# Three buffers instead of two for the stacked queries of a cross-attention stage

## The reference

```
x = layernorm(x + self_part(x))      # causal exp(q k^T) row sums, then a 1 -> 16 -> 512 MLP
x = layernorm(x + cross(x))          # 16 heads of 32, 154 keys per sequence
x = layernorm(x + ffn(x))            # int16-like activations, int8-like weights, 512 -> 2048 -> 512

cross: q, k, v = heads(x), heads(ctx), heads(ctx)
       weights = softmax((q k^T + bias) / sqrt(32)); out = (weights v) @ w_out
```

## Time and profile before

| | |
|---|---|
| median of 3 runs | 2299.92 us (2289.78 to 2301.79) |
| profiled execution | 2294.64 us |
| its span, first to last instruction | 2292.8 us |
| busy PE / DVE / ACT / POOL | 2126.1 / 1737.9 / 1086.0 / 827.0 us |
| share of the chain that ended last: PE / DVE / DMA / ACT | 82% / 6% / 4% / 2% |
| of it the DMA `qs<-stack` | 3% |
| mean granted TensorE clock | 0.947 |

### The profile page before, as it was taken

How to read it: one execution, slowest core, us unless ns; L and a number is a source line. 1 busy time by engine, 2 the same in 40 slices (tenths; PEclk the granted TensorE clock), 3 DMA queues, 4 the chain that set the end, 5 groups by cost and what they waited for, 6 DMA issues and landing times.

```text
span 2292.8 us, 32921 instructions
## 1 busy us (share of the span) xinstructions
PE 2126.1 (93%) x11880; PEld 1185.0 (52%) x11904; DVE 1737.9 (76%) x3296; ACT 1086.0 (47%) x1522; POOL 827.0 (36%) x802
## 2 busy tenths in 40 slices
PE   7999999984998999999999859999999699999997
PEld 3444444431776777777777624444444344444443
DVE  6768686865677897898898665777666488888885
ACT  1444444442454555555555324444444465555551
POOL 2122221222134555455555342222222134444442
PEclk9999999996588999999999779999999899999999
DMA  6344343457769979989995437888888656667662
GB/s 232 107 132 148 99 145 107 115 137 187 172 147 181 269 165 201 265 182 180 262 193 141 155 84 255 287 283 288 271 268 273 244 200 232 225 227 235 227 224 79
DMA packets 386626, 448.46 MB, mean 196 GB/s; under 512 B 279270, under 2 KB 279430, under 8 KB 368032
## 3 DMA queue, kind: packets, MB, share of 16 engines
q1 hardware_dynamic: 322448, 286.07, 46.4%
q0 software_dynamic: 64016, 160.28, 22.6%
HBM read 258.93 MB, written 138.73 MB: 173 GB/s over the span
## 4 chain that ended last, share of the span: by engine, by line
PE 82%; DVE 6%; issue 5%; DMA 4%; ACT 2%; POOL 1%; SPq 0%; DVEq 0%; POOLq 0%; ACTq 0%
PE ps_h L1704 19%; PE ps L1947 19%; PE ps_proj L600 10%; PE ps_o L1272 8%; PE ps_w L1301 6%; PE ps_s L620 5%; PE ps_o L1268 3%; DMA qs<-stack 3%; PE ps_m L1224 3%; PE ps_m L1226 3%; PE ps_l L1250 3%; DVE rope_t L428 1%; PE ps_t L1286 1%; PE ps_l L1247 1%; DVE x_hi L411 1%
## 5 line engine op out<-in xcount | busy, mean ns | idle before, releaser
L1704 PE MATMUL ps_h<-xT,b_rows 128*128 128x512 f16 x2048 | 444.5, 380 | 12.7 <-DMA xT<-x_lo 12.7
L1947 PE MATMUL ps<-w,g_hi 128*128 128x512 f16 x1024 | 389.1, 380 | 21.7 <-DVE g_lo L1883 21.7
L1947 PE MATMUL ps<-w,g_lo 128*128 128x512 f16 x1024 | 389.0, 380 | 0.0
L1704 PEld LDWEIGHTS ps_h<-xT,b_rows 128*128 128x128 f16 x2048 | 200.8, 98 | 256.1 <-issue 16.0
L1272 PEld LDWEIGHTS ps_o<-vm,pT 128*128 128x128 f32 x2048 | 308.9, 208 | 14.7
L1545 ACT ACTIVATE h<-ps_h,b_in_sb,col_scale 128x512 f32<-128x512 f32 x256 | 199.5, 779 | 240.8 <-PE ps_h L1704 240.6
L1096 DVE TENSOR_REDUCE stack<-ps_m 128x2 f16<-128x308 f32 x512 | 244.1, 478 | 78.1 <-PE ps_m L1226 75.9
L1272 PE MATMUL ps_o<-vm,pT 128*128 128x33 f32 x2048 | 292.4, 269 | 0.0
L1047 ACT ACTIVATE pT<-logit 128x512 f32<-128x512 f32 x320 | 199.2, 624 | 131.0 <-DVE logit L1114 130.0
L1618 DVE TENSOR_REDUCE amax_t<-h 128x1 f32<-128x2048 f32 x64 | 146.2, 2284 | 118.3 <-ACT h L1545 118.1
L1796 POOL TENSOR_TENSOR rstd<-vare,minus_half 128x1 f32<-128x1 f32 x64 | 154.3, 2411 | 208.4 <-DVE vare L1901 208.4
(11 more groups left out here) (179 smaller groups left out, 3935.5 us busy)
## 6 DMA issues: line engine op xcount, KB each, us to landing
hidden<-h POOLq DMA_DIRECT2D x64, 1024.0 KB, 6.8
hT<-hidden SPq DMA_DIRECT2D x64, 1024.0 KB, 6.1
xc<-x_cols SPq DMA_DIRECT2D x16, 1024.0 KB, 5.1
xr<-x_rows SPq DMA_DIRECT2D x16, 1024.0 KB, 5.5
x_rows<-x POOLq DMA_DIRECT2D x16, 1024.0 KB, 4.8
x1t<-x_rows SPq DMA_DIRECT2D x64, 256.0 KB, 3.8
bt_main<-bias_main SPq DMA_DIRECT2D x16, 1024.0 KB, 6.9
xres<-x_rows SPq DMA_DIRECT2D x64, 256.0 KB, 3.8
```

What stands on the lines that cost most here:

```text
L1704: mm = pe.matmul(ps_h[f % 4][:], w1[:, c, f * P:(f + 1) * P], xT[:, e, a, :, c, :], start=(a == 0 and c == 0), stop=(a == 1 and c == KC - 1))
L1947: mm = pe.matmul(ps[t][:], g[:, e, f, t * P:(t + 1) * P], w2[:, f, :], start=(f == 0 and a == 0), stop=(f == FC - 1 and a == 1))
```

## The change: a third buffer, and where its room comes from

`stack` gets a third buffer: tile t uses buffer t % 3, and its writers wait for the transpose of tile t-3. There are three semaphores `st_in`, and a helper `stack_turned(eng, tile)` that waits for one tile's transpose. Nothing else in the order of work is changed: each engine issues the same instructions in the same order.

The room: `ident_f` becomes a view of the first 512 B of `wo_hi`, which is written much later; ten small tensors of the stage become views of one tensor `misc`; the small tensors of the third stage become views of the last, unused part of `b_rows`. As `b_rows` is in use until the last maxima, the load of `b_in` (one small DMA on SP near the end of the stage) now waits for them. DVE's one clearing of `stack` covers three buffers instead of two. Addresses shift: `stack` starts at byte 73,728 of a partition instead of 74,592, `q16` at 86,016 instead of 82,784, `qs` at 16,768 instead of 17,632.

```
-        ident_f, ident_h, b_rows, bt_main = shared.ident_f, shared.ident_h, shared.b_rows, shared.bt_main
+        ident_h, b_rows, bt_main = shared.ident_h, shared.b_rows, shared.bt_main
-        stack = sb("stack", [P, 2, HEADS, P], F16)
+        stack = sb("stack", [P, 3, HEADS, P], F16)
+        ident_f = wo_hi[:, 0, 0:2 * P].bitcast(F32)
+        misc = sb("misc", [P, 39], F32)
+        minus_half, bn_spacer, spacer = misc[:, 0:1], misc[:, 1:2], misc[:, 2:3]
...
-        st_in = pair("st_in")
+        st_in = [sem(f"st_in{i}") for i in range(3)]
+        def stack_turned(eng, tile):
+            eng.wait_ge(st_in[tile % 3], 16 * (tile // 3 + 1))
 # turn_stack, SP
                 sp.dma_start_transpose(qs[:, n % 2, :, t * P:(t + 1) * P],
-                                       stack[:, t % 2].rearrange("p h d -> p (h d)")).then_inc(st_in[t % 2], 16)
+                                       stack[:, tile % 3].rearrange("p h d -> p (h d)")).then_inc(st_in[tile % 3], 16)
 # stack_halves, ACT (low_half on POOL and maximum on DVE alike)
-                if not (isinstance(tile, int) and tile < 2):
-                    act.wait_ge(st_in[t % 2], 16 * (2 * nu + t // 2))
+                if tile >= 3:
+                    stack_turned(act, tile - 3)
 # logits, PE
-                    pe.wait_ge(st_in[0], 32 * (n + 1))
-                    pe.wait_ge(st_in[1], 32 * (n + 1))
+                    for tile in range(4 * n + 1, 4 * n + 4):
+                        stack_turned(pe, tile)
 # third stage, SP
                     if g == 0:
+                        sp.wait_ge(tail.mx_ready, 8 * 4 * NBLK)
                         sp.dma_start(b_in_sb[:], b_in).then_inc(consts_in, 16)
 # build
+        spare = b_rows[:].rearrange("p t h k -> p (t h k)")[:, KC * FF:].bitcast(F32)
+        shared = Lasting(ident_h=ident_h, b_rows=b_rows, bt_main=bt_main, b_in_sb=spare[:, 0:F], amax1=spare[:, F:2 * F],
...
```

More of the change, by code:

```diff
@@ L670, in self_attention_stage @@
                              pieces=BATCH * NPIECE, last=last)
-Lasting = namedtuple("Lasting", "ident_f ident_h amax_run b_in_sb amax1 w_scale col_scale ax_all x_scale b_rows bt_main")
+Lasting = namedtuple("Lasting", "ident_h amax_run b_in_sb amax1 w_scale col_scale ax_all x_scale b_rows bt_main")
 CrossAttentionTail = namedtuple("CrossAttentionTail", "sp pool act dve pe quarters first biased lg_done mx_ready amax_part "
@@ L711, in cross_attention_stage @@
         wo_lo = sb("wo_lo", [P, KC, DIM], F16)
-        minus_half = sb("minus_half2", [P, 1], F32)
+        ident_f = wo_hi[:, 0, 0:2 * P].bitcast(F32)
+        misc = sb("misc", [P, 39], F32)
+        minus_half, bn_spacer, spacer = misc[:, 0:1], misc[:, 1:2], misc[:, 2:3]
+        vare, rstd = misc[:, 3:5], misc[:, 5:7]
+        mv = misc[:, 7:11].rearrange("p (e k) -> p e k", e=2)
+        bn = misc[:, 11:23].rearrange("p (e k) -> p e k", e=2)
+        rsum = misc[:, 23:39].rearrange("p (c t h) -> p c t h", c=2, t=2)
         vm = sb("vm", [P, 2, HEADS, VW], F32)
@@ L717, in cross_attention_stage @@
         pT = sb("pT", [P, 2, 5, BLK], F32)
-        rsum = sb("rsum", [P, 2, 2, 4], F32)
         comb = sb("comb", [P, 2, 2, P], F32)
@@ L724, in cross_attention_stage @@
         y = sb("y2", [P, 2, DIM], F32)
[L725 to L729, removed]
         x2t = sb("x2t", [P, 2, DIM], F32)
         amax_t = sb("amax_t", [P, 4 * UNITS], F32)
-        spacer = sb("spacer", [P, 1], F32)
         ps_m = [ctx.enter_context(nc.psum_tensor(f"ps_m{i}", [P, 512], F32)) for i in range(2)]
@@ L952, in low_half @@
                 pool.wait_ge(q16_ready, tile + 1)
-                if not (isinstance(tile, int) and tile < 2):
-                    pool.wait_ge(st_in[t % 2], 16 * (2 * (4 * s + b) + t // 2))
-                pool.tensor_tensor(stack[:, t % 2, :, 2 * HD:3 * HD],
+                if tile >= 3:
+                    stack_turned(pool, tile - 3)
+                pool.tensor_tensor(stack[:, tile % 3, :, 2 * HD:3 * HD],
                                    x1t[:, t % 2].rearrange("p (h d) -> p h d", d=HD),
@@ L1033, in stack_halves @@
                 tile = 4 * nu + t
-                if not (isinstance(tile, int) and tile < 2):
-                    act.wait_ge(st_in[t % 2], 16 * (2 * nu + t // 2))
+                if tile >= 3:
+                    stack_turned(act, tile - 3)
                 x = x1t[:, t % 2].rearrange("p (h d) -> p h d", d=HD)
-                act.activation(stack[:, t % 2, :, 0:HD], x, ACT.Copy)
-                act.activation(stack[:, t % 2, :, HD:2 * HD], x, ACT.Copy).then_inc(high_ready, 1)
+                act.activation(stack[:, tile % 3, :, 0:HD], x, ACT.Copy)
+                act.activation(stack[:, tile % 3, :, HD:2 * HD], x, ACT.Copy).then_inc(high_ready, 1)
             def weights(n, g, k):
@@ L1093, in maximum @@
                 dve.wait_ge(mx_done, 8 * tile + k + 1)
-                if k == 0 and not (isinstance(tile, int) and tile < 2):
-                    dve.wait_ge(st_in[t % 2], 16 * (2 * nu + t // 2))
-                dve.tensor_reduce(stack[:, t % 2, 2 * k:2 * k + 2, 3 * HD], ps_m[k % 2][:, 0:2 * KEYS].rearrange(
+                if k == 0 and tile >= 3:
+                    stack_turned(dve, tile - 3)
+                dve.tensor_reduce(stack[:, tile % 3, 2 * k:2 * k + 2, 3 * HD], ps_m[k % 2][:, 0:2 * KEYS].rearrange(
                     "p (h k) -> p h k", h=2), AX.X, ALU.max, negate=True).then_inc(mx_ready, 1)
@@ L1978, in build @@
                                     bias_rows, b_rows, rows_in, block, sems)
[L1979 to L1984, removed]
+        ident_h = lasting("ident_h", [P, P], F16)
+        bt_main = lasting("bt_main", [P, GROUPS, 4, BLK], F32, side="right")
+        spare = b_rows[:].rearrange("p t h k -> p (t h k)")[:, KC * FF:].bitcast(F32)
+        F = FF // P
+        shared = Lasting(ident_h=ident_h, b_rows=b_rows, bt_main=bt_main, b_in_sb=spare[:, 0:F], amax1=spare[:, F:2 * F],
+                         w_scale=spare[:, 2 * F:3 * F].rearrange("p (g c) -> p g c", c=4), col_scale=spare[:, 3 * F:4 * F],
+                         amax_run=spare[:, 4 * F:4 * F + 1], ax_all=spare[:, 4 * F + 1:4 * F + 2],
+                         x_scale=spare[:, 4 * F + 2:4 * F + 3])
         tail = cross_attention_stage(nc, x1_rows, ks_dram, kb_dram, v_main, v_tail, bias_rows, bias_main, bias_tail, w_out,
```

## The result

The changed kernel takes 2269.36 us (median of 4 executions, 2262.12 to 2284.26) against 2294.85 us of the kernel before (median of 4): ratio 0.9899, 95% interval 0.9857 to 0.9940. It is faster, by 25.5 us between these medians where 23.3 were worked out from the profile, and its time lies inside the range. Measured again later (five executions beside new ones of before) the ratio was 0.9927 (0.9898 to 0.9955); the median of all nine executions is 2277.0 us, 17 to 18 under the two medians that before had beside them (2294.2 and 2294.9).

The account below looks back on a forecast made before the run. PE, 82% of the chain, was held up by ACT's waits for the stack's transpose. Of 44.5 us too long at seven places, 23.3 would be gained: 2294.6 less 23.3 is 2271.3, called 2272, range 2254 to 2288.

Parts of the forecast that it names:

- The writers of the stack wait for tile t-3: Second stage: ACT's 46.8 us of waits for the stack's transpose all go, and POOL's and DVE's with them.
- Next is the cast: ACT's cast in the bursts then waits for `x1t`, starting 0.7 us earlier than before; the next stack transpose follows 2.0 us later.
- A: 692.7 to 726.7 us, two quarters 13.2 us too long; PE wait of 6.3 and clock 3.3 stay, 3.6 gained.
- Three waits at unit starts after A, C and E: PE waits for late stack transposes before the logits: 6.3, 2.0 and 3.0 us, each with 3.3 more for the clock.
- C: 888.0 to 903.8 us, quarter 5.4 us too long; PE wait of 2.0, with the clock 5.3, stays; 0.1 gained.
- E: 1056.9 to 1084.8 us, two quarters 7.1 us too long; PE wait of 3.0, with the clock 6.3, stays; 0.8 gained.
- all stalls go: Rival, 14%: the boundary transposes come in time too, no PE wait at unit starts; 44.5 us gained, 2250 us.
- F: 1116.3 to 1132.2 us, quarter 5.5 us too long; the next transpose comes in time, all 5.5 gained.
- The price of the clock: After a PE wait of this size the granted clock falls to 0.50, costing 3.3 us beyond the wait's length.
- The rival of the DMA pace: Rival, 20%: DMA engines set the bursts' pace, loads brought forward lengthen the next transposes; 10 us gained, 2285 us.
- The addresses: Rival, 9%: `stack` starting at a multiple of 256 bytes speeds its transposes, 8.1 us to 6.0; 9.5 us more, 2262 us.
- slower: Rival, 7%: boundary transposes after three places get later, 8.7 us becoming 16.5 ends the gain; 11 us on each gives 2304.

Follow-up runs that it names:

- e1: Changed kernel's layout with three buffers allocated but only two used, writers waiting for tile t-2: 2281.78 us, ratio 0.9957 to the kernel before.
- e2: Changed kernel with SP loading the residual `xres` one quarter earlier: 2272.64 us, ratio 0.9910 to the kernel before.
- e7: The changed kernel itself run again, for a second profile: 2277.6 us, ratio 0.9927 to the kernel before.
- e3: Changed kernel with the `x1t` and `xres` loads issued ahead of the stack's transpose on SP, `xres` one quarter early: 2290.07 us, ratio 1.0000 to before.
- e8: Changed kernel with the `x1t` and `xres` loads issued by ACT instead of SP, `xres` one quarter early: 2280.16 us, ratio 0.9931 to before.
- e9: Kernel before, two buffers, without the twelve later `b_rows` loads (later row maxima wrong): 2263.96 us, ratio 0.9882 to before.
- e10: Changed kernel, three buffers, without the twelve later `b_rows` loads (later row maxima wrong): 2253.09 us, ratio 0.9835 to before.
- e5: Kernel before, two buffers, moved by 160 bytes so `stack`, `q16` and `x1t` start at multiples of 256 bytes: 2283.0 us, ratio 0.9941 to before.
- e6: Changed kernel with the stage's tensors moved by 32 bytes, so `stack` starts 32 past a multiple of 256: 2279.8 us, ratio 0.9934 to before.
- e12: Changed kernel with `vm` and `vt` loaded two quarters later where they meet `b_rows`, and `xres` one quarter early: 2265.27 us, ratio 0.9871 to before.

## Why the prediction was right, and where it was not

*The writers of the stack wait for tile t-3: all waits of ACT go.* Right: 46.8 us became none, PE's 17.7 for the exponentials none; with e1's two buffers both came back (39.4 and 11.5).

*Next is the cast, waiting for `x1t`, 0.7 us earlier than before.* Right in kind: 44.1 us in 19 waits. Its size at place A was better than forecast. Three rows of SP's and ACT's timeline there, and the landing time of the last:

```profile
700.27 0.52 SPq L851 DMA_DIRECT2D x1t<-x_rows  x1
...
707.42 0.63 ACT L1030 ACTIVATE q<-x1t 128x512 f16<-128x512 f32 x1 [3.50 <-DMA x1t<-x_rows]
...
709.44 4.70 SPq L840 DMA_TRANSPOSE qs<-stack  x1
...
qs<-stack SPq DMA_TRANSPOSE x1, 9.2
```

The cast started at 707.4 (forecast 709.7), the transpose 2.0 us behind it as forecast, and it landed at 709.4 + 9.2 = 718.7 (forecast 719.8); the logits followed at 718.8. Undisturbed they would have been at 695.4 + 20.8 = 716.2. The unit started 2.7 us late, and the transpose was only the last 0.15 us of PE's waiting; the first was for `y`:

```profile
709.32 0.59 PE L1304 MATMUL ps_w<-wo_hi,combT 128*128 128x512 f16 x2 [0.79 <-DVE y L1145]
...
718.86 0.40 PE L1250 MATMUL ps_l<-qs,ks 97*32 97x512 f16 x4 [0.15 <-issue]
```

Without the short waits ahead of it PE would have stood some 2.5 us for this transpose (718.7 less 716.2, an estimate), still not 6.3. And the granted clock stayed at 1.00 from 708 to 724 us, so the 3.3 us for it weren't paid either.

*Three waits at unit starts after A, C and E, each with 3.3 us of clock.* This is the step that failed. PE's waits for the logits' transposes come to 0.2 us in both profiles of the changed kernel, where 6.3, 2.0 and 3.0 were forecast. The prediction's own sign for this was "then all stalls go"; they did not. The prediction followed one reader of the late loads, the cast and the transpose behind it. It left out the second: `xres`, issued by SP in the same breath, needed through `y` and the one `ps_w` buffer, and late in the same burst. The trace of the kernel before had it, as the waits of 577 to 1250 us and a row of DVE's timeline at place A show:

```profile
DVE y L1142 <- issue: 26.1, 8, 6.4
...
710.54 0.69 DVE L1142 SCALAR_TENSOR_TENSOR y<-ps_w,xres 128x512 f32<-128x512 f32 x1 [6.44 <-issue]
```

`y` started within 0.1 us of PE's release from its wait for `weights` 4 (710.51): the stack's wait hid this one. At C it was PE's wait (5.35 us) and came before the logits'. Behind A it makes one too, of 2.64 us, and a quarter of 17.6. The forecast waits appeared only once `xres` was moved away (e2: 2.7, 1.7 and 2.1 us). At F, forecast free, two rows show a third way from the cast to PE: ACT stood 4.5 us for `x1t`, `combT` stands behind the cast on ACT, and PE waited for it.

```profile
1106.73 0.63 ACT L1030 ACTIVATE q<-x1t 128x512 f16<-128x512 f32 x1 [4.51 <-DMA x1t<-x_rows]
...
1108.29 0.59 PE L1304 MATMUL ps_w<-wo_hi,combT 128*128 128x512 f16 x2 [1.47 <-ACT combT L1067]
```

So the sum came out near (15.4 us in the stretch where 23.3 were forecast, 25.5 between the medians) with terms that didn't: A and E gave more (10.5 and 6.2 us where 3.6 and 0.8 were forecast), C and F less, and the quarters behind A gave 8.1 back. In e7 the stretch gave 10.9, less than half of the forecast. That the total agrees is partly luck.

*The price of the clock, 3.3 us a wait.* It is no fixed price. After the wait at C the engines' row reads 0.50 again (last columns: granted clock, DMA share, GB/s), the level of 1.2 GHz:

```profile
892.00:896.00 4.00, 2.62 (x7) 0.92 (x8) 3.37 (x9) 1.60 (x3) 0.00 (x0) 0.50 1.62 197
```

C: 5.35 us of waiting made a quarter 7.8 too long, 2.4 beyond the waiting; behind A 2.64 and a short wait of 0.65 made 7.2, 3.9 beyond; at F 1.47 and 0.65 made 5.7, 3.6 beyond. F's wait is a quarter of C's and its quarter lost three quarters as much. At A the kernel before had made 13.2 out of 5.53. After the change, 0.79 and 0.65 made a quarter of 12.8 us, 2.4 too long, and none of that is the clock's, which stayed at 1.00. The dearest is in e7: a wait of 2.51 and one of 0.65, after which the clock stayed at 0.50 to the end of the quarter. It took 20.8 us, 7.2 beyond the waiting.

```profile
901.14 0.59 PE L1304 MATMUL ps_w<-wo_hi,combT 128*128 128x512 f16 x2 [2.51 <-DVE y L1145]
...
902.00:906.00 4.00, 3.40 (x15) 2.55 (x15) 3.97 (x11) 1.55 (x3) 0.00 (x0) 0.50 1.24 197
...
914.00:918.00 4.00, 4.00 (x18) 2.23 (x18) 1.90 (x4) 0.00 (x0) 0.00 (x0) 0.50 0.65 163
```

So one row could not give the price of the others, and the clock is likely part of why executions of one kernel differ.

*The rival of the DMA pace* (given 20%) was right as a mechanism. The share above is 1.62 where it was 1.33, though over 870 to 920 us the profiles read 1.12 (before), 1.29 (after) and 1.15 (e7); a share says that the DMA engines are busy, not that their queues take turns. e3 and e8 show that whoever gets its data sooner takes it from another; e9 and e10 show what the burst costs. Its price, a gain of 10 us, is not ruled out by the stretch (15.4 and 10.9 us in the two profiles); the medians, 17 to 25 us apart, speak for more.

*The addresses* (given 9%) are real: 4.3 us became 3.7, and e5 shows 0.4 to 0.6% from them alone. The prediction gave the landing times 2.1 us under load for this; that was too much, and the 2272 left it out altogether. How it shares the gain with the third buffer stays open: e1, e5, e6 and e7 have intervals that overlap.

*All stalls go*, and *slower*: not seen. The longest transpose was 14.2 us (12.6 in e7) where 16.5 would have been needed, against 13.5 before.

*The clearing, forecast 1.3 us and hidden:* the row reads

```profile
L1159 DVE MEMSET stack<- x1: 1298/1298/1298, 517.9 to 517.9; 128x1488 f16 x1
```

*What stays open.* The executions of one kernel lie 25 us apart (2262.1 to 2287.1 for the changed kernel), more than the prediction allowed for. Part of this falls ahead of the bursts: the first of the 48 quarters starts anywhere from 679.7 to 701.4 us. The changed kernel's first profile has a stall there that before's and e7's have not:

```profile
608.38 0.69 DVE L1173 TENSOR_SCALAR wo_hi<-y 128x1024 f16<-128x1024 f32 x1 [9.87 <-DMA x2t<-w_out]
```

PE waits 4.3 and 4.9 us in it (602 and 612 us), so the two profiled executions of before and after don't differ by the change alone. The profiles of e2, e6 and e12 have it too (8.8 to 10.6 us), those of e5 and e9 a shorter one (6.9 and 2.8). Why it comes in some executions was not tried.

## What to carry to other kernels

One more buffer takes away the waits for the buffer; before you count the gain, list every load that is in flight in the same burst and every engine that reads one, not only the first in the program's order, because the wait moves to the next late one. Where moving loads between places and queues only changes who waits, put fewer or later bytes into the burst: fewer helped here (e9, e10), later gave the lowest median of the kernels that do all the work (e12), which its interval doesn't secure. Don't take the cost of a slow clock from one wait to another: here it was anything from nothing to some 7 us. And when an edit changes the layout of memory, measure the layout by itself, with the old logic in the new layout and the other way round.

## What the runs showed of the hardware

- DMA transposes out of a buffer that starts at a multiple of 256 bytes, into one at a multiple of 128, landed in 3.6 or 3.7 us at the shortest (512 KB; e3 apart), against 4.3 us from 32 or 96 bytes past one, into one 32 past a multiple of 64; those into `q_heads` (128 KB) in 2.3 us against 2.4, in all kernels of either kind. Moving the stage's tensors of the kernel before by 160 bytes gave a ratio of 0.9941, or 0.9964 between the medians of all executions.
- Loads that ACT issued in place of SP did not land sooner (e8: `x1t` 4.5 us from issue to landing at the median, 13.5 at most, against 3.8 and 10.3 in the changed kernel and 3.9 and 9.5 in e2). The Trainium skill, DMA: Bandwidth & Descriptors (Rules for kernel authors), says that spreading DMAs over issuing engines brings no bandwidth. By that rule, e8 agrees.
- Transposes of the stack that take 5.7 us at the median took up to 14.2 us beside the bulk loads (5.3 and 17.5 in e3), so a wait that is sized by the median misses what costs the time.
- TensorE's granted clock after waits of like size: 0.50 for the rest of a quarter after 2.51 and 0.65 us (e7, 902 to 918 us), back at 1.00 from 878 us on after 2.41 us (e7, waiting until 875 us), and 1.00 throughout after 0.79 and 0.65 us (after, 708 to 724 us).
